# Holding x doubled and moving part of the residual sum from VectorE to GpSimd in a macaron block

## What is computed

```python
x = x + 0.5 * ffn(layernorm(x))         # tanh(((n @ W1) @ W2) @ W3 + b)
x = x + linear_attention(layernorm(x))  # elu features, 16 heads, out * z @ Wo + bo
x = x + 0.5 * ffn(layernorm(x))
x = x + 0.5 * spectral(layernorm(x))    # real(ifft(fft(n) @ w)) + bias
x = x + softmax_attention(layernorm(x)) # 16 heads of 64, causal
x = x + 0.5 * spectral(layernorm(x))

def layernorm(x, eps=1e-5):
    return (x - mean(x)) / sqrt(var(x) + eps)
```

## Time and profile before

| | |
|---|---|
| Median of 3 runs | 1256.41 us (1256.25 to 1256.64) |
| The profiled execution | 1257.7 us |
| Its span | 1254.8 us |
| TensorE busy | 1187.8 us, 95% |
| VectorE busy | 1023.7 us, 82% |
| ScalarE busy | 1002.5 us, 80% |
| GpSimd busy | 587.4 us, 47% |

### The profile page before, as it was taken

One profiled execution on the slowest core, in us unless ns is written; L12 is line 12 of the kernel. 1 busy time (PEld: TensorE's weight loads), 2 busy tenths in 40 slices (PEclk: granted clock), 3 DMA queues, 4 the chain that ended last, 5 costly groups with the idle time before them and its releaser, 6 DMA issues.

```text
span 1254.8 us, 38244 instructions
## 1 busy us (share of the span) xinstructions
PE 1187.8 (95%) x10824; PEld 1035.2 (83%) x10824; DVE 1023.7 (82%) x4874; ACT 1002.5 (80%) x3489; POOL 587.4 (47%) x912
## 2 busy tenths in 40 slices
PE   5699977789999999999999999999999999999996
PEld 4689966778888888888888888888888888888885
DVE  6888879977888888888888888888888888888874
ACT  4777648678888888888888888888888888888883
POOL 4822138634444444444444444444444444444442
PEclk9999999999999999999999999999999999999998
DMA  7000000000000000000000000000000000000000
GB/s 223 1 2 0 1 2 1 1 2 2 2 11 0 8 0 8 0 8 0 8 0 8 0 8 0 8 0 8 0 8 0 8 0 8 0 8 0 10 2 18
DMA packets 14540, 11.79 MB, mean 9 GB/s; under 512 B 725, under 2 KB 12569, under 8 KB 14489
## 3 DMA queue, kind: packets, MB, share of 16 engines
q1 hardware_dynamic: 14336, 11.19, 3.0%
q10 hardware_dynamic: 152, 0.00, 0.0%
HBM read 7.00 MB, written 4.19 MB: 9 GB/s over the span
## 4 chain that ended last, share of the span: by engine, by line
PE 82%; DVE 8%; issue 3%; POOL 2%; ACT 2%; DVEq 0%; DMA 0%; POOLq 0%; SPq 0%; ACTq 0%
PE ps L1115 15%; PE ps L1098 13%; PE ps L1124 10%; PE ps L1084 7%; PE ps L1067 7%; PE ps L1080 6%; PE ps L1068 5%; PE ps L1069 5%; PE ps L1106 2%; PE ps L1104 2%; PE ps L1105 2%; DVE bst L413 2%; POOL rstd L318 1%; DVE xn L426 1%; PE ps L1140 1%
## 5 line engine op out<-in xcount | busy, mean ns | idle before, releaser
L809 ACT ACTIVATE pr<-ps,neg_max 128x128 f32<-128x128 f32 (+1 forms) x1024 | 424.5, 429 | 111.4 <-DVE neg_max L527 111.4
L333 POOL TENSOR_TENSOR pr<-pr,rinv 128x256 f32<-128x256 f32 x256 | 157.4, 615 | 514.3 <-DVE rinv L535 514.3
L527 DVE CUSTOM_DVE_ANT_0 ps<-ps,mask 128x128 f32<-128x128 f32 (+1 forms) x1024 | 329.8, 392 | 0.4
L335 POOL TENSOR_TENSOR pr<-pr,rinv 128x512 f32<-128x512 f32 x256 | 266.2, 1040 | 0.0
L542 DVE COPY pT<-ps 128x512 f32<-128x512 f32 x256 | 176.2, 688 | 61.2 <-PE ps L1098 59.9
L809 ACT ACTIVATION_READ_ACCUMULATOR pr<-ps,neg_max 128x1 f32 x1024 | 217.8, 213 | 0.0
L1098 PE MATMUL ps<-ident,pr 128*128 128x128 f32 x1536 | 210.2, 273 | 2.2 <-POOL pr L335 0.9
L1115 PE MATMUL ps<-pT,space 128*64 128x256 f32 (+1 forms) x2048 | 196.2, 334 | 0.7 <-ACT pT L818 0.5
L1098 PEld LDWEIGHTS ps<-ident,pr 128*128 128x128 f32 x1536 | 179.4, 141 | 20.8 <-POOL pr L335 2.1
L1115 PEld LDWEIGHTS ps<-pT,space 128*64 128x64 f32 x2048 | 127.4, 137 | 56.0 <-issue 0.8
L1067 PE MATMUL ps<-x_hi,wqk_hi 128*128 128x256 f32 x512 | 167.8, 328 | 1.6 <-DVE x_lo L507 1.1
(11 more groups left out here) (173 smaller groups left out, 2622.7 us busy)
## 6 DMA issues: line engine op xcount, KB each, us to landing
...
```

What stands on the lines that cost most here:

```text
L333: nc.gpsimd.tensor_tensor(pr[:, buf, :, 0, :], pr[:, buf, :, 0, :], r[:, :, 0:1].to_broadcast([P, 2, P]), ALU.mult)
L335: nc.gpsimd.tensor_tensor(pr[:, buf, :, 1:3, :].rearrange("p h b k -> p h (b k)"), pr[:, buf, :, 1:3, :].rearrange("p h b k -> p h (b k)") ...
L527: last = nc.vector.tensor_tensor_reduce(o, o, mask[:, T - w:T], -1.0, -MASKED, ALU.add, ALU.min, neg_max[:, j, 2 * h + qt:2 * h + qt + 1])
L809: last = nc.scalar.activation(dst, ps[:, BANK_S + 2 * j + h, qt * P:qt * P + w], ACT.Exp, bias=neg_max[:, j, at:at + 1], scale=-1.0, accum ...
```

## The change

x is held doubled from the first residual sum on. FFN1 adds as `2 * x + tanh`. LIN's output is doubled by halving its denominators and doubling its output bias. FFN2 then adds its tanh as it is, and SPEC1 its whole product, with a circulant and a bias that aren't halved. The softmax output has twice the scale, and the last sum halves x again and uses a halved circulant and a halved bias. Since x is doubled, epsilon is four times as large in every norm after the first.

In FFN2 and SPEC1 the sum is now divided: DVE adds the first tile of a group, and POOL the other three, once DVE has added its tile. POOL can't take the product from PSUM, so in SPEC1 ACT first copies it into `th`. POOL keeps the power alone of its four small operations; DVE adds epsilon (`variance`) and makes the shift from mean and power in one operation (`minus_mean`); the negated mean is gone. In DVE's turn the sum now stands first instead of last, and shift and variance stand last. The inverse deviations of softmax batches 0 and 1 move in POOL's queue to before its turns 14 and 15 of SPEC1, so that they stand behind its sums of groups 13 and 14.

```diff
@@ constants, tiles
-OUT_SCALE = 1.0 / H
+OUT_SCALE = 2.0 / H
+EPS_2X = 4.0 * EPS
+half_circ = sb("half_circ", [P, D])
-bias_bf = sb("bias_bf", [P, 5 * D], BF16)
+bias_bf = sb("bias_bf", [P, 6 * D], BF16)
@@ POOL
+nc.gpsimd.memset(eps_2x[:], EPS_2X)
+def power(phase):
+    def f(g, j):
+        n = g + phase * G
+        pool.wait_ge(veps_ready, count(g + ((phase - 2) * G + 1)))
+        pool.wait_ge(xn_ready, count(n - 1))
+        pool.wait_ge(xn_act_ready, count(n - 1))
+        nc.gpsimd.tensor_tensor(rstd[:, j, :], veps[:, j, :], half_neg[:], ALU.pow).then_inc(rstd_ready, 1)
+    return f
+def add_th(phase, k):
+    def f(g, j):
+        pool.wait_ge(th_ready, count(g + (k * G + 1)))
+        pool.wait_ge(x_part_ready, count(g + ((phase - 2) * G + 1)))
...
+        nc.gpsimd.tensor_tensor(xg(g, 1, GT - 1), xg(g, 1, GT - 1), th[:, j, D:], ALU.add).then_inc(x_ready, 1)
+    return f
-phases(pool, [[(5, g_inv_std(phase))] for phase in (FFN1, LIN, FFN2, SPEC1)])
+phases(pool, [[(5, g_inv_std(FFN1))], [(5, g_inv_std(LIN))], [(0, add_th(FFN2, 1)), (5, power(FFN2))],
+              [(0, add_th(SPEC1, 2)), (5, power(SPEC1))]],
+       early={(3, G - 2): lambda: inv_std(SOFT, 0, BT, eps_2x, 2 * G), (3, G - 1): lambda: inv_std(SOFT + 1, 1, BT, eps_2x, 2 * G + 1)})
-inv_std(SOFT, 0, BT)
-inv_std(SOFT + 1, 1, BT)
@@ DVE
+nc.vector.tensor_scalar(bias_bf[:, HALF_FFT_B:HALF_FFT_B + D], bias_bf[:, FFT_B:FFT_B + D], 0.5, None, ALU.mult)
-    nc.vector.scalar_tensor_tensor(out=xg(g), in0=th[:, j, :], scalar=0.5, in1=xg(g),
+    nc.vector.scalar_tensor_tensor(out=xg(g), in0=xg(g), scalar=2.0, in1=th[:, j, :],
+def variance(phase):
+        dve.wait_ge(mv_ready, count(g + (phase * G + 1)))
+        nc.vector.tensor_scalar(veps[:, j, :], mv[:, j, :, 1], EPS_2X, None, ALU.add).then_inc(veps_ready, 1)
+def minus_mean(phase):
+        dve.wait_ge(rstd_ready, count(n + 1))
+        dve.wait_ge(xn_act_ready, count(n - 1))
+        nc.vector.scalar_tensor_tensor(out=shift[:, j, :], in0=mv[:, j, :, 0], scalar=-1.0, in1=rstd[:, j, :],
+                                       op0=ALU.mult, op1=ALU.mult).then_inc(shift_ready, 1)
+def add_part(k):
+        dve.wait_ge(th_ready, count(g + (k * G + 1)))
+        nc.vector.tensor_tensor(xg(g, 0, 1), xg(g, 0, 1), th[:, j, 0:D], ALU.add).then_inc(x_part_ready, 1)
-nc.vector.tensor_scalar(den[:], num_den[:, :, P:P + H0], Z_EPS, None, ALU.add).then_inc(den_ready, 1)
+nc.vector.tensor_scalar(den[:], num_den[:, :, P:P + H0], Z_EPS, 0.5, ALU.add, ALU.mult).then_inc(den_ready, 1)
-nc.vector.tensor_tensor(xb(b), ps[:, BANK_X, BT * D:], xb(b), ALU.add).then_inc(out_ready, 1)
+nc.vector.scalar_tensor_tensor(out=xb(b), in0=xb(b), scalar=0.5, in1=ps[:, BANK_X, BT * D:],
+                               op0=ALU.mult, op1=ALU.add).then_inc(out_ready, 1)
-             [(3, g_norm(FFN2)), (5, g_stats(FFN2)), (0, add_tanh(1))],
-             [(3, g_norm(SPEC1)), (5, g_stats(SPEC1)), (0, add_bank(mm_done, 3 * G, lambda j: BANK_OUT + j))]],
+             [(0, add_part(1)), (3, g_norm(FFN2)), (5, g_stats(FFN2)), (4, minus_mean(FFN2)), (5, variance(FFN2))],
+             [(0, add_part(2)), (3, g_norm(SPEC1)), (5, g_stats(SPEC1)), (4, minus_mean(SPEC1)), (5, variance(SPEC1))]],
@@ ACT
-    nc.scalar.mul(circ[:], ps[:, 2, D:2 * D], 0.5 / D).then_inc(su_ev, 1)
+    nc.scalar.mul(half_circ[:], ps[:, 2, D:2 * D], 0.5 / D)
+    nc.scalar.mul(circ[:], ps[:, 2, D:2 * D], 1.0 / D).then_inc(su_ev, 1)
+def spectral_out(g, j):
+    act.wait_ge(mm_done, count(g + (3 * G + 1)))
+    act.wait_ge(x_ready, count(g + (3 * G - 1)))
+    nc.scalar.copy(th[:, j, :], ps[:, BANK_OUT + j, :]).then_inc(th_ready, 1)
-             [(2, xT_out(SPEC1)), (3, act_norm(SPEC1))]],
+             [(2, xT_out(SPEC1)), (3, act_norm(SPEC1)), (1, spectral_out)]],
@@ PE
-            [(2, transpose(SPEC1)), (1, product(SPEC1, circ[:], FFT_B, x_ready, 3 * G))]],
+            [(2, transpose(SPEC1)), (1, product(SPEC1, circ[:], FFT_B, th_ready, 2 * G))]],
```

More of the change, by code:

```diff
@@ L136, in build @@
         rows = sb("rows", [1, 5 * D])
-        FFN_B, FFT_B, BO_B, KV_B = 0, D, 2 * D, 3 * D
+        FFN_B, FFT_B, BO_B, KV_B, HALF_FFT_B = 0, D, 2 * D, 3 * D, 5 * D
         space = sb("space", [P, 2 * BT * H * DV + 2 * PAIRS * T])
@@ L305, in _, with inv_std @@
             POOL0 = 4
-            def inv_std(n, j, w):
+            def inv_std(n, j, w, eps, step):
                 pool.wait_ge(mv_ready, count(n + 1))
@@ L1137, in spectral_product @@
                 mm(o.rearrange("p (t d) -> p t d", d=D), ones_bf[:, 0:P],
-                   bias_bf[:, FFT_B:FFT_B + D].unsqueeze(1).to_broadcast([P, BT, D]), start=True, stop=False, skip_group_check=True)
+                   bias_bf[:, HALF_FFT_B:HALF_FFT_B + D].unsqueeze(1).to_broadcast([P, BT, D]), start=True, stop=False, skip_group_check=True)
                 for t in range(BT):
-                    last = mm(o[:, t * D:(t + 1) * D], z_xT[:, t * P:(t + 1) * P], circ[:], start=False, stop=True,
+                    last = mm(o[:, t * D:(t + 1) * D], z_xT[:, t * P:(t + 1) * P], half_circ[:], start=False, stop=True,
                               skip_group_check=True)
```

27 lines of the change are left out of this document (18 added, 9 removed).

## The result

The changed kernel takes **1267.82 us** (median of five runs, 1264.24 to 1269.58) against 1256.41 (1255.99 to 1257.04): 1.0084 of the time before, interval 1.0069 to 1.0100. The forecast was 1261.3 with a range to 1265.0. The direction was right, the size was not: +11.4 us measured, +4.9 forecast. The profiled execution took 1267.82 us with a span of 1265.0.

A forecast was written before the change was run, and what follows sets the result against it. It took a ring between ScalarE and TensorE, not VectorE, to bound the two stages. Terms 0.35 + 0 + 0.25 + 3.2 + 1.1 = +4.9 us on the 1256.4 median gave 1261.3, range 1256.8 to 1265.0.

The forecast's parts named there:

- The bound, and the steady turns at 0: FFN2 and SPEC1 steady turns: ScalarE and TensorE set the pace, VectorE is late for nobody, so the change costs 0.
- VectorE saves 0.14 a turn: FFN2 and SPEC1: VectorE's shorter sum saves 0.38 us, two small operations and a wait cost 0.24; bounds -0.18 and +0.38.
- the ring: FFN2 and SPEC1: ScalarE's xT copy and normalisation and TensorE's transposes follow each other, 2.22 us a turn, 2.29 mean.
- the slack of 0.87: FFN2, a turn outside the hardware loop: VectorE's half of a group was normalised 0.87 us before TensorE's transposes.
- Shift's order of waits: FFN2 and SPEC1: POOL's sum falls beside VectorE's one-input statistics; the new waits use up slack at most once per stage.
- the third rival: FFN2 and SPEC1: VectorE and GpSimd exclude each other, a 2.5 us loop, 5.6 us over 28 turns, about 1267; chance 0.10.
- End of the spectral stage, +3.2: End of SPEC1: softmax batches' inverse deviations queue behind POOL's sums, delaying the first query and key product; bounds +2.7, +3.7.
- GpSimd's sum 0.83: FFN2 and SPEC1: POOL's 128x384 sum takes 0.83 us, by a straight line between two sizes; bounds 0.615 and 1.04.
- TensorE's clock +1.1: After SPEC1's end: TensorE's granted clock falls to 0.50 after the gap, costing 1.1 us; bounds 0 and 1.3.
- Linear to FFN boundary +0.25: Boundary from LIN to FFN2: two small operations before the context mask lengthen VectorE's chain by 0.25 us; bounds 0 and 0.56.
- Start +0.35: Kernel start: a second circulant copy on ScalarE, 0.2, and a bias halving on VectorE, 0.15; bounds 0 to 0.56.
- Softmax part 0: Softmax part: the last sum becomes a two-operator form over the same elements, other changes are constants; cost 0.

The follow-up runs named there:

- e7: Changed kernel with GpSimd's sum cut from 128x384 elements to 128x1 in FFN2 and SPEC1, all waits kept, residual incomplete; 1262.57 us.
- e13: Changed kernel with GpSimd's sum cut to 128x1 elements and negated mean, epsilon, power and shift all back on GpSimd; 1259.37 us.
- e9: Changed kernel with VectorE's hardware loop over four turns instead of two, the other engines' loops unchanged; 1267.14 us.
- e2: Changed kernel with the inverse deviations of softmax batches 0 and 1 one turn earlier in GpSimd's queue, ahead of the sums of groups 13 and 14; 1265.28 us.
- e3: Changed kernel with VectorE's two small operations exchanged, epsilon added before shift is made; 1268.61 us.
- e5: Changed kernel with VectorE's sum of tile 0 at the end of its turn and GpSimd's power ahead of its sum; 1265.37 us.
- e12: Changed kernel with VectorE's sum last in its turn, SPEC1 groups 13 to 15 summed by VectorE alone, and every engine's loop over four turns; 1262.29 us.
- e10: Kernel before the change, with every engine's hardware loop over four turns; 1258.17 us.
- e1: Changed kernel with x held doubled, but every sum, epsilon, mean and shift on its old engine in the old order; 1256.83 us.
- e4: Changed kernel with the halved circulant and halved bias made later, so nothing new stands before the first transposes; 1267.45 us.

## Why the prediction was right and wrong

- **The bound, and the steady turns at 0: wrong, and the largest error.** The failed step was "VectorE saves 0.14 a turn ... and the ring doesn't ask for it". Its terms were -0.38 for the sum and +0.24 for two small operations. Measured: -0.26 and +0.385 (5.51 - 4.74, and 4.99 - 5.51, by two), so VectorE's turn grew by 0.125. The small operations were mis-sized, and the sum's relief lost 0.12 to a branch that no term had (it costs 0.32 each second turn behind 0.16 us of epsilon, 0.52 against 0.20 from start to start, and cost 0.13 before). Together they lie within the stated bound of -0.18 a turn. But I had read the slack of 0.87 in a turn outside the loop. Inside, VectorE's 2.37 stood beside the ring's 2.33: no slack was being made there. Cost: FFN2 +2.72, of which e7 leaves 0.76 to VectorE's own turn and takes 1.96 with GpSimd's sum, and SPEC1 +0.55, which e7 and e13 both clear: it is the sum's collisions, come when VectorE's lead is spent.
- **Shift's order of waits: wrong.** "By the order of waits POOL's sum falls beside statistics" holds at the start of the sum. It ends beside shift, and in turns without statistics shift, the norm and the sum are released by the same power. This is the mechanism of the third rival (0.10), at the edges and not in each turn; its loop of 2.5 us is 2.4 in e9. That its total, 1267, is close to the 1267.8 measured is luck: it puts 5.6 us into the steady turns, where 3.3 were lost. Its chance was set on one row, while the negated means of FFN2 showed the exclusion in eight turns.
- **End of the spectral stage, +3.2: right in its reason and near in size (3.54).** The chain gave 2.5 for batch 0 and 0.7 for batch 1; measured are 2.73 and 0.81. With GpSimd's sum at 1.00 instead of 0.83, twice, it would have given 3.5. What it didn't contain is the second chain, VectorE's lost lead (1.62 at the statistics of batch 0): it lies under the queue and added 0.11, but with the norms held beside the sums it is why taking the queue away in e2 gave back 1.05 and not 3.5.
- **GpSimd's sum 0.83: 1.00**, near its bound of 1.04. A straight line between two sizes of another operation was no guide.
- **TensorE's clock +1.1: 1.41**, over its bound of 1.3, and 2.4 in e3 and e9 behind the same 7.08. The bound rested on a low clock of 2.7 us in the earlier trace rows; over 176 to 184 us of that trace the mean granted clock is 0.79, which is 3.4 us at 0.50. In e13 a gap of 5.35 cost nothing and in e7, with TensorE idle the same 2.93 us before the product, 1.34, so it isn't given by the gap.
- **Linear to FFN boundary +0.25:** the kernels with the small operations on VectorE have 39.62 to 39.82 us, apart from e3, e5 and e12, those without 39.16 to 39.28: +0.45, inside the bounds. The step to xT copy 2 is 2.91 and 2.88 in the kernel before and e10, and 3.07 to 3.82 in the fourteen that hold x doubled, e1 among them. Their clock is low there for longer (mean 0.57 over 178 to 186 us in the changed kernel, 0.79 over 176 to 184 before). No experiment shows why.
- **Start +0.35:** not to be told from 0 in the scatter (e1, e4). The 1.95 of the profile were falls of the clock that executions of the same instructions have or don't have.
- **Softmax part 0:** right, +0.08.

What of the 11.4 us stays open: the account gives 9.1 without the +1.95 at the start and the -0.88 at SPEC1's start (a fall of the clock at 218 to 222 us that of these two executions only the one before has), neither of them set by the change. For the remaining 2.3 us between the medians the spans and mean granted clocks of all runs say more. The five runs of the changed kernel have 0.990 on the mean, and 57 runs of the kernel before beside the experiments 0.992, with a median of 1256.8. At equal clocks, 0.990 and 0.991, the changed kernel's spans are 1265.0 and 1264.4 and those of the kernel before 1256.2 and 1255.8 on the mean: 8.7 us, where the account has 7.7 without the 1.41 of the clock. So part of the 2.3 is the clock, and what stays unexplained is nearer 1 us; that is an estimate from five runs of the changed kernel.
